# A top-64 attention kernel: VectorE writes the copy below the pivot and the final mask, GpSimd and the excess pass leave the group loop

## The reference, cut to what matters

```python
q = (x @ Wq)...; k, v = split(x @ Wkv)             # 16 heads of 64
k = concatenate([mem_k, k]); v = concatenate([mem_v, v])   # 16 memory columns ahead
dots = einsum('bhid,bhjd->bhij', q, k) * SCALE
dots = einsum('bhij,hk->bkij', dots, pre_proj)     # heads are mixed
dots = where(causal, NEG_INF, dots)
thresh = top_k(dots, 64)[0][..., -1:]              # the 64th largest of each row
dots = where(dots < thresh, NEG_INF, dots)
attn = softmax(dots, axis=-1)
out = einsum('bhij,bhjd->bhid', attn, v) ...
```

## Time and profile before

| | us |
|---|---|
| median of 3 runs (3874.14 to 3875.96) | 3874.56 |
| the profiled execution | 3873.98 |
| its span | 3872.1 |
| TensorE busy | 2315.0 |
| VectorE busy | 2245.1 |
| ScalarE busy | 1712.3 |
| GpSimd busy | 1674.8 |
| first pivots to the start of the last (63 periods) | 3137.5 |

### The profile page before, as it was taken

How to read it: one execution, slowest core, us unless ns; L and a number is a source line. 1 busy time by engine, 2 the same in 40 slices (tenths; PEclk the granted TensorE clock), 3 DMA queues, 4 the chain that set the end, 5 groups by cost and what they waited for, 6 DMA issues and landing times.

```text
span 3872.1 us, 34819 instructions
## 1 busy us (share of the span) xinstructions
PE 2315.0 (60%) x10182; PEld 1329.5 (34%) x10182; DVE 2245.1 (58%) x8918; ACT 1712.3 (44%) x2399; POOL 1674.8 (43%) x554
## 2 busy tenths in 40 slices
PE   5885445455556666336666675766660467673598
PEld 3553222233323333113333333333330234342365
DVE  3245776666665666775555555655579556451444
ACT  1212334444445555225555556555540555654221
POOL 0000233434455455235566557666640666757000
PEclk9896667777777878668787887888885788786799
DMA  1000000000000000000000000000000000000100
GB/s 46 1 1 1 1 1 1 1 1 1 1 1 1 1 1 1 0 1 1 1 1 1 1 1 1 1 1 1 1 1 0 1 1 1 1 1 1 38 1 11
DMA packets 15487, 12.02 MB, mean 3 GB/s; under 512 B 6892, under 2 KB 13686, under 8 KB 15222
## 3 DMA queue, kind: packets, MB, share of 16 engines
q1 hardware_dynamic: 11184, 6.82, 0.7%
q10 hardware_dynamic: 4038, 2.37, 0.2%
HBM read 8.14 MB, written 1.05 MB: 2 GB/s over the span
## 4 chain that ended last, share of the span: by engine, by line
DVE 35%; POOL 31%; PE 14%; issue 9%; ACT 8%; DVEq 3%; ACTq 0%; POOLq 0%
POOL F L425 26%; DVE W L1159 6%; POOL R L432 5%; DVE W L1160 4%; DVE r L1176 4%; DVE cand L1137 3%; PE bank L939 3%; DVE r L1208 3%; ACT R L566 3%; DVEq L1212 2%; ACT R L573 2%; DVE Pm L1221 2%; ACT R L558 2%; PE bank L947 2%; PE bank L857 1%
## 5 line engine op out<-in xcount | busy, mean ns | idle before, releaser
L425 POOL TENSOR_SCALAR F<-R,thr 128x144 bf16<-128x144 f32 (+15 forms) x256 | 1022.4, 3994 | 1246.8 <-DVEq L1171 1217.7
L841 PE MATMUL bank<-ident,R 128*128 128x128 f32 x2176 | 552.2, 327 | 1289.0 <-ACT R L573 1289.0
L432 POOL TENSOR_TENSOR R<-R 128x144 f32<-128x144 f32 (+15 forms) x256 | 647.2, 2528 | 655.3 <-ACT R L566 650.3
L841 PEld LDWEIGHTS bank<-ident,R 128*128 128x128 f32 x2176 | 356.5, 164 | 1540.7 <-issue 790.0
L857 PE MATMUL bank<-WP,Y 128*128 128x512 f32 x1088 | 667.6, 701 | 79.8 <-ACT WP L580 77.9
L573 ACT ACTIVATE R<-R,negm 128x144 f32<-128x144 f32 (+15 forms) x256 | 310.2, 1213 | 882.7 <-POOL F L425 882.0
L1137 DVE MAX8 cand<-R 128x8 f32<-128x12 f32 (+15 forms) x4096 | 558.7, 222 | 31.8 <-ACT R L543 13.0
L1176 DVE MAX8 r<-R 128x8 f32<-128x144 f32 (+15 forms) x256 | 334.0, 1306 | 404.6 <-POOL R L432 404.6
L825 PE MATMUL bank<-hT,qT 128*128 128x512 f32 (+3 forms) x1280 | 519.3, 540 | 28.9 <-ACT R L539 15.3
L842 PE MATMUL bank<-nidentb,F 128*128 128x128 bf16 x2176 | 484.3, 247 | 0.0
L543 ACT ACTIVATE R<-bank 128x1024 f32<-128x1024 f32 (+7 forms) x384 | 290.5, 774 | 379.2 <-PE bank L825 221.2
(11 more groups left out here) (219 smaller groups left out, 2287.4 us busy)
## 6 DMA issues: line engine op xcount, KB each, us to landing
R<-in_L_attn_Wkv ACTq DMA_DIRECT2D x2, 512.0 KB, 8.1
R<-in_L_ffn_gate_w SPq DMA_DIRECT2D x1, 1024.0 KB, 6.8
R<-in_L_ffn_up_w SPq DMA_DIRECT2D x1, 1024.0 KB, 9.4
out<-X SPq DMA_DIRECT2D x1, 1024.0 KB, 5.1
R<-in_L_attn_Wq ACTq DMA_DIRECT2D x1, 512.0 KB, 6.5
WP<-in_L_attn_Wo ACTq DMA_DIRECT2D x1, 512.0 KB, 10.9
R<-in_L_ffn_wi SPq DMA_DIRECT2D x1, 256.0 KB
R<-in_L_ffn_wo SPq DMA_DIRECT2D x1, 256.0 KB
```

The source lines that it names most:

```text
L425: pool.tensor_scalar(F[:, i, 0:n], S[:, k % NS, i, 0:n], thr[:, k % 2, i:i + 1], 4.0, ALU.is_lt, ALU.mult).then_inc(s_lose, 1)
L432: pool.tensor_tensor(A[:, u % 2, 0:n], S[:, p % NS, i, 0:n], A[:, u % 2, 0:n], ALU.subtract) .then_inc(s_below, 1)
L841: pe.transpose(to[:, P * i:P * i + P], S[:, k % NS, i, blk], ident[:, :])
```

## The change

GpSimd's loop and with it the semaphores `s_over`, `s_below` and `s_thr` are taken out; GpSimd keeps only the constants at the start. ScalarE's `excess` is taken out; its counts write their signs, which nobody reads, into row 0 of `A`. VectorE's `below` now writes the copy itself, in one instruction a tile: the score, less 1.0 where the score is above the cut. So that 1.0 is a huge number, all scores are scaled by `LOW` = 2^-30 through the constant `pre_b`, the causal mask is -1.0, `BIG_` goes to 2^90, and the exponential scales back. `r9` has the cut itself in front of the eight, so that a count of 64 has its threshold too; the tie term still looks at column 1, which now is the first of the eight. `threshold` ends with the four masks F, written by VectorE behind the branch. `memory_weights` moves ahead of the searches. On ScalarE all four exponentials come first, then three turns, then the four counts with a turn's drain behind each, then the other drains; the scores of group p+2 are drained at the end of iteration p (where those of p+1 were drained at its start).

The diff, without its changes of constants on GpSimd and of the branch's row of `A`:

```diff
@@ -19,16 +19,17 @@
 EPS = 1e-5
-FILL = -2.0 ** 30
+LOW = 2.0 ** -30
+FILL = -1.0
 NS = 3
 SC = 1024
-BIG_ = 2.0 ** 60
+BIG_ = 2.0 ** 90
 RANGE = 60000.0
...
 CUT = 56
-CONSTS = 3 + 2 * E0 + 9
+CONSTS = 4 + 2 * E0 + 9
 GU = 4
@@ -184,9 +185,9 @@
         W16 = sb("W16", [P, 2, 8 * CH * GU], F16)
-        r8 = sb("r8", [P, GU, 8])
-        hit = sb("hit", [P, GU, 8])
-        place = sb("place", [P, 8])
+        r9 = sb("r9", [P, GU, 9])
+        hit = sb("hit", [P, GU, 9])
+        place = sb("place", [P, 9])
         top = sb("top", [P, GU])
@@ -194,7 +195,7 @@
         idx = sb("idx", [P, GU])
-        thr = sb("thr", [P, 2, GU])
+        thr = sb("thr", [P, GU])
         tie = sb("tie", [P, GU])
@@ -310,10 +311,7 @@
         s_cnt = sem("s_cnt")
-        s_over = sem("s_over")
-        s_below = sem("s_below")
         s_eight = sem("s_eight")
-        s_thr = sem("s_thr")
         s_lose = sem("s_lose")
@@ -408,28 +407,6 @@
             pool.tensor_scalar(nidentb[:, :], ident[:, :], -1.0, None, ALU.mult).then_inc(s_const, 1)
-
-            for p in range(NG + 1):
-                if p >= 1:
-                    k = p - 1
-                    n = wide(k // 4)
-                    pool.wait_ge(s_thr, k + 1)
-                    if p < NG:
-
-                        pool.wait_ge(s_cut, p + 1)
-                    if k:
-
-                        pool.wait_ge(s_tfill, turned(k - 1))
-                        pool.wait_ge(s_pm, k)
-                    for i in range(GU):
-                        pool.tensor_scalar(F[:, i, 0:n], S[:, k % NS, i, 0:n], thr[:, k % 2, i:i + 1], 4.0, ALU.is_lt,
-                                           ALU.mult).then_inc(s_lose, 1)
-                if p < NG:
-                    n = wide(p // 4)
-                    for i in range(GU):
-                        u = GU * p + i
-                        pool.wait_ge(s_over, u + 1)
-                        pool.tensor_tensor(A[:, u % 2, 0:n], S[:, p % NS, i, 0:n], A[:, u % 2, 0:n], ALU.subtract)                            .then_inc(s_below, 1)
@@ -552,25 +529,17 @@
                 n = wide(k // 4)
-                if u >= 2:
-                    act.wait_ge(s_eight, u - 1)
+                if u:
+                    act.wait_ge(s_cnt, u)
                 act.wait_ge(s_cut, k + 1)
-                act.activation(A[:, u % 2, 0:n], S[:, k % NS, i, 0:n], ACT.Sign, bias=cutb[:, k % 2, i:i + 1], scale=BIG_,
+                act.activation(A[:, 0, 0:n], S[:, k % NS, i, 0:n], ACT.Sign, bias=cutb[:, k % 2, i:i + 1], scale=BIG_,
                                accum_out=cnt[:, k % 2, i:i + 1]).then_inc(s_cnt, 1)
-
-            def excess(k, i):
-
-                u = GU * k + i
-                n = wide(k // 4)
-                act.wait_ge(s_cnt, u + 1)
-                act.activation(A[:, u % 2, 0:n], S[:, k % NS, i, 0:n], ACT.Relu, bias=cutb[:, k % 2, i:i + 1], scale=BIG_)\
-                    .then_inc(s_over, 1)
...
                 row = S[:, k % NS, i, 0:n]
-                act.activation(row, row, ACT.Exp, bias=negm[:, k % 2, i:i + 1], scale=1.0).then_inc(s_prob, 1)
+                act.activation(row, row, ACT.Exp, bias=negm[:, k % 2, i:i + 1], scale=1.0 / LOW).then_inc(s_prob, 1)
@@ -590,29 +559,25 @@
             drain_scores(0)
+            drain_scores(1)
             for p in range(NG + 1):
-                if p + 1 < NG:
-                    drain_scores(p + 1)
+                turns = list(range((p - 1) // 4 + 1)) if p >= 1 else []
                 if p >= 1:
-                    exponent(p - 1, 0)
-                    exponent(p - 1, 1)
+                    for i in range(GU):
+                        exponent(p - 1, i)
+                    for j in turns[0:3]:
+                        drain_turn(p - 1, j)
                 if p < NG:
-                    count_above(p, 0)
-                    excess(p, 0)
+                    for i in range(GU):
+                        count_above(p, i)
+                        for j in turns[3 + i:4 + i]:
+                            drain_turn(p - 1, j)
                 if p >= 1:
-                    exponent(p - 1, 2)
-                    exponent(p - 1, 3)
-                turns = (p - 1) // 4 + 1 if p >= 1 else 0
-                ahead = [(f, i) for i in range(1, GU) for f in (count_above, excess)] if p < NG else []
-                for j in range(turns):
-                    while ahead and 10 * (7 - len(ahead)) <= 12 * j + 10:
-                        f, i = ahead.pop(0)
-                        f(p, i)
-                    drain_turn(p - 1, j)
-                for f, i in ahead:
-                    f(p, i)
-                if p >= 1:
+                    for j in turns[7 if p < NG else 3:]:
+                        drain_turn(p - 1, j)
                     drain_rest(p - 1)
+                if p + 2 < NG:
+                    drain_scores(p + 2)
@@ -1083,7 +1048,7 @@
                     dve.wait_ge(s_wa, 16 * 9)
-                    link(dve.tensor_scalar(pre_b, pre_b, DH ** -0.5, None, ALU.mult))
+                    link(dve.tensor_scalar(pre_b, pre_b, DH ** -0.5 * LOW, None, ALU.mult))
             dve.wait_ge(s_dve, done[0])
@@ -1141,8 +1106,8 @@
                 mark(dve.tensor_reduce(top[:, :], cand[:, 0].rearrange("p l u -> p u l"), AX.X, ALU.max))
-                link(dve.tensor_scalar(W16[:, 0, :], cand[:, :, :, :].rearrange("p r l u -> p (r l u)"), -RANGE, RANGE,
-                                       ALU.max, ALU.min))
+                link(dve.tensor_scalar(W16[:, 0, :], cand[:, :, :, :].rearrange("p r l u -> p (r l u)"), 1.0 / LOW, -RANGE,
+                                       ALU.mult, ALU.max))
                 flip, runs = 0, 8
@@ -1164,30 +1129,35 @@
                 link(dve.tensor_reduce(piv[:, :], dst.rearrange("p r u -> p u r"), AX.X, ALU.min))
-                mark(dve.tensor_scalar(negm[:, k % 2, :], top[:, :], -1.0, None, ALU.mult))
-                link(dve.tensor_scalar(cutt[:, :], piv[:, :], -BIG_ * (1 - NEAR), None, ALU.mult))
-                link(dve.scalar_tensor_tensor(out=cutb[:, k % 2, :], in0=piv[:, :], scalar=-BIG_ * (1 + NEAR),
+                mark(dve.tensor_scalar(negm[:, k % 2, :], top[:, :], -1.0 / LOW, None, ALU.mult))
+                link(dve.tensor_scalar(cutt[:, :], piv[:, :], -BIG_ * LOW * (1 - NEAR), None, ALU.mult))
+                link(dve.scalar_tensor_tensor(out=cutb[:, k % 2, :], in0=piv[:, :], scalar=-BIG_ * LOW * (1 + NEAR),
                                               in1=cutt[:, :], op0=ALU.mult, op1=ALU.max))
...
             def below(k, i):
-                u = GU * k + i
-                dve.wait_ge(s_below, u + 1)
-                dve.max(r8[:, i, :], A[:, u % 2, 0:wide(k // 4)]).then_inc(s_eight, 1)
+                u, n = GU * k + i, wide(k // 4)
+                row = S[:, k % NS, i, 0:n]
+                if i == 0:
+                    link(dve.tensor_scalar(r9[:, :, 0], cutb[:, k % 2, :], -1.0 / BIG_, None, ALU.mult))
+                link(dve.scalar_tensor_tensor(out=A[:, 1, 0:n], in0=row, scalar=r9[:, i, 0:1], in1=row, op0=ALU.is_gt,
+                                              op1=ALU.subtract, reverse1=True))
+                dve.max(r9[:, i, 1:9], A[:, 1, 0:n]).then_inc(s_eight, 1)
+                dve.wait_ge(s_eight, u + 1)
...
                 n = wide(t)
-                th = thr[:, k % 2, :]
+                th = thr[:, :]
                 dve.wait_ge(s_cnt, GU * k + GU)
...
                 link(dve.tensor_scalar(idx[:, :], cnt[:, k % 2, :], -0.5, TOPK - n / 2 + 0.25, ALU.mult, ALU.add))
-                mark(dve.scalar_tensor_tensor(out=tie[:, :], in0=r8[:, :, 1], scalar=-BIG_, in1=cutb[:, k % 2, :],
+                mark(dve.scalar_tensor_tensor(out=tie[:, :], in0=r9[:, :, 1], scalar=-BIG_, in1=cutb[:, k % 2, :],
                                               op0=ALU.mult, op1=ALU.is_le))
                 link(dve.tensor_scalar(idx[:, :], idx[:, :], HALF, -HALF, ALU.add, ALU.add))
-                link(dve.tensor_tensor(hit[:, :, :], place[:, :].unsqueeze(1).to_broadcast([P, GU, 8]), bc(idx[:, :], 8),
+                link(dve.tensor_tensor(hit[:, :, :], place[:, :].unsqueeze(1).to_broadcast([P, GU, 9]), bc(idx[:, :], 9),
                                        ALU.is_equal))
-                link(dve.tensor_tensor(hit[:, :, :], hit[:, :, :], r8[:, :, :], ALU.mult))
+                link(dve.tensor_tensor(hit[:, :, :], hit[:, :, :], r9[:, :, :], ALU.mult))
                 link(dve.tensor_reduce(th, hit[:, :, :], AX.X, ALU.add))
@@ -1203,16 +1173,21 @@
                     for i in range(GU):
-                        s_, a_, m_ = S[:, k % NS, i, 0:n], A[:, 0, 0:n], r8[:, i, :]
+                        s_, a_, m_ = S[:, k % NS, i, 0:n], A[:, 1, 0:n], r9[:, i, 1:9]
                         for r in range(8):
...
                                 dve.drain()
-                        dve.tensor_copy(thr[:, k % 2, i:i + 1], m_[:, 7:8])
+                        dve.tensor_copy(thr[:, i:i + 1], m_[:, 7:8])
```

(12 more changed lines are left out.)

5 lines of the change are left out of this document (3 added, 2 removed).

## The result

The changed kernel takes 3443.79 us (median of three runs, 3438.75 to 3448.46) against 3874.56 us: a ratio of 0.8887 with a 95% interval of 0.8867 to 0.8908, so 431 us less. The forecast was 3360 with a range of 3320 to 3500. The time lies 84 us above the forecast, on a rival with its price: one more exact search.

What follows compares the result with a forecast made beforehand. Hand-overs between engines, mainly VectorE and GpSimd, were taken to bound the kernel. VectorE's 2652 us, plus 30 for ScalarE and TensorE and 77 for the tail, gave a 2759 us loop against 3273.2, 514 less: 3360 us, range 3320 to 3500.

Steps and rivals of the forecast that it cites:

- the first rival: Exact-search branch: one score equal to the cut triggers it, some 45 to 145 us, 3455 and up; chance 0.32.
- What bounds it: Whole loop: hand-overs between engines, not a full engine (none busy over 60% of the span), bound the kernel before.
- VectorE's period: VectorE's steps for a group of four rows, n columns wide: 22.2 + 14/960 n us, 46.7 at 1680.
- The 34 us: VectorE between last search and next pivots: some 15 of 63 periods take 2.26 us more, 34 us in all.
- Pm at 0.21: L1221 on VectorE, moved ahead of the searches, takes 0.21 us; the other end is 1.46, 79 us more in all.
- The two old exact searches: Rare branch behind L1204, groups 34 and 55: both kernels take it there, 89.6 + 129.6 = 219 us.
- The case named likeliest: Whole kernel: the forecast of 3360 us, with exact searches in two groups only; chance 0.50.
- no single score equal to a cut: Flag's tie term: no row triggers another branch; 0.49 such rows expected in 32,768, chance 0.38 for one or more.
- The chain of ScalarE and TensorE: Exponentials, turns, counts, scores: 57.5 us at 2064 columns, 3.4 less a step, adding 30 us over the last four widths.
- The lower clock: TensorE at 0.50 through the counts: its chain binds from 1296 columns, about 95 us more, 3455; chance 0.07.
- The tail: From the last pivots to the end of the loop: 77 us, was 135.7.
- The sum: VectorE's 63 periods: 1399 + 1000 + 219 + 34 = 2652 us, plus 30 for ScalarE and TensorE.

Runs made afterwards that it cites:

- experiment 4b: Changed kernel with the masks F back on GpSimd and Pm behind the four copies and searches, ahead of the threshold: 3780.91 us, ratio 0.9758.
- experiment 5: Changed kernel with ScalarE's excess pass and GpSimd's subtraction making the copy again, F staying on VectorE and Pm early: 3731.22 us, ratio 0.963.
- experiment 1: Changed kernel with the tie term at column 2 of r9 again and no threshold ready for a count of 64: 3342.5 us, ratio 0.8624.
- experiment 3: Changed kernel without flag read and exact search, copy and top-8 search covering only the first half of each row: 2918.4 us, ratio 0.7534.
- experiments 4: Changed kernel with F on GpSimd again and Pm between the third and fourth search, the copy staying on VectorE: 3891.29 us, ratio 1.0045.
- experiment 2: Changed kernel with the flag neither read nor branched on, so without the exact search: 3031.04 us, ratio 0.7819.
- experiment 8: Changed kernel with the tie rule of before, plus the next group's fourth search moved between the flag and its reading: 3287.85 us, ratio 0.8486.

## Why the prediction was right, and where it was off

- **What bounds it.** Right. The stalls at the hand-overs went, not the sum of GpSimd's busy time. VectorE sets the period in 59 of 63, that is up to the third group at 1936 columns.
- **VectorE's period** (22.2 + 14n/960) held within 0.1 us in the plain groups of most widths: 26.1, 27.9, 29.8, 33.5, 37.3, 41.0, 44.7 and 46.6 us at 272, 400, 528, 784, 1040, 1296, 1552 and 1680 columns, against 26.2, 28.0, 29.9, 33.6, 37.4, 41.1, 44.8 and 46.7 by the sum. Copy and mask were priced from neighbours with another shape and pointer count, and both prices hold to 0.01 us. At 144 columns it didn't: 22.6 to 26.7 against 24.3. The 34 us for some 15 periods with 2.26 us more were about right: 13 of the 63 have 3.6 to 3.9 us from flag to mask where the others have 1.4, some 30 us.
- **Pm at 0.21** was right, with 0.226. The Trainium skill's rule on the shared port pair (SBUF — State Buffer, Who interferes with whom), which the forecast named beside this end, agrees: in the kernel before, the long Pm at 2590.32 ended at 2592.47 us, and the L432 that it met at 2592.38. Experiments 4b and 5 show other VectorE instructions that get longer beside GpSimd, in 4b by less than the rule has it.
- **The two old exact searches** stayed, in groups 34 and 55, as the count of scores above the pivots said. Their prices in the changed kernel are 91.3 and 131.0 us from flag to mask, beside the 91.06 and 131.09 to the pivots in the earlier trace rows.
- **The case named likeliest didn't happen.** The step that failed is "no single score equal to a cut", which had 0.50 against 0.32 for one or more. Group 40 has one, at 1424 columns, and pays 107.3 - 1.4 = 106 us. This was the first rival: its mechanism, with a price of 45 to 145 us by width, is what happened, and experiment 1 shows it by taking the term back. The range held because it took that rival in. Scores computed in double precision, as I had them, tell the counts above a cut but not whether the chip's own f32 scores come out equal to it.
- **The chain of ScalarE and TensorE** was mis-sized in what it adds. The forecast gave it 57.5 us at 2064 and 3.4 less a step, and added 30 us for the last four widths. Its own length was nearly right: experiment 3 shows means of 54.8, 53.0, 46.2 and 37.5 us at 2064, 1936, 1680 and 1296 columns, where the forecast's step gives 57.5, 54.1, 47.3 and 37.1. What it adds to the loop is some 14 us: one period of 54.1 at 1936, and 55.8, 55.4 and 57.8 at 2064 (the last with 2.3 of a slow flag read) against VectorE's 50.4 and 52.3. At 1808 it is 49.1 and not 50.7, so hardly longer than VectorE's 48.4. At 1936 it is 53.4 to 54.9 in the changed kernel too, but the exact search of group 55 had let ScalarE catch up, and the first three groups use that up. The forecast had no such term. The scores, taken as 18.3 us from the earlier trace rows, take 16.9 at 2064 (3039.47 to 3056.34). The stretch in the earlier trace rows has a drain of queries (L532, 0.60 us, and more wait for the next bank) among the scores; this one has none, and with one it is 18.2 at 1936 in both kernels. The whole is 55.5 where 57.5 was forecast.
- **The lower clock** was a rival if it lasted through the counts. It is 0.50 for some 10 us, from about 2 us after the start of the exponentials to just before the first count, and 1.00 from 3070 on, while the counts run. So only the first turns pay.
- **The tail** from the last pivots to the end of the loop was forecast at 77 us. The line that the earlier trace rows ends with is, in the changed kernel,

```profile
3186.98 3.19 DVE L941 BATCH_NORM_STATS2 st<-WP 128x6 f32<-128x128 f32 x16
```

  at 3186.98, 78.4 us after 3108.6.
- **The sum.** 63 periods: 2682 forecast, with the third search 2788, measured 2769.9; the 18 less are mostly the chain's 30, found as some 14. Outside the loop and in the tail the rest agrees within 2 us.
- **My expectations of experiments 4 and 5** failed by 190 and 250 us (and that of 4b by 80), far more than the forecast of the change itself. Both times I summed the engines' work and one wait, and didn't ask what was queued behind the waiting instruction: four copies behind Pm, and the turns' drains behind the counts.

So the gain doesn't split into a part for the mask and one for the copy. With the mask alone back on GpSimd the kernel takes 3781 to 3891 us, with the copy alone back 3731, with both in place but ScalarE's order taken back 3656. From 3875 to 3444 it takes all three; each half keeps one ring of hand-overs alive. These times all hold the third exact search, some 105 us that the kernel before hasn't. Less that, as an estimate, the change is worth 532 us (experiment 1), and with the mask back 87 to 198 of them are left, with the copy back 248, with ScalarE's order back 324.

## What to carry to other kernels

When an engine's work in a loop is cheap to redo on the engine that waits for it, price the move by the waits at the hand-over, not by busy times: here 537 us more work on VectorE (186.2 + 350.3) gave 431 us, and 532 without the third exact search. Ask for every wait that stays what stands behind it in its queue, on both engines. A fast path with a rare exact branch has to be costed with its trigger: a term that was loosened from two equal scores to one cost 101 us, almost a quarter of what the change gained. Such a search also stays in every comparison with the kernel before, until it is taken out of both sides.

## What the hardware showed that I had not expected

- Reading a flag into a register and branching costs VectorE 1.19 us of idle time in each group, and a little over 2 us more in 14 of the 64; both go when the branch goes (experiment 2). When another instruction of 2.8 us runs meanwhile, the 1.19 us go, but 1.1 to 2.6 us are left in 23 groups (experiment 8).
- A VectorE instruction of 128x4 elements took 1.18 us on average in experiment 5, up to 4.25 where it met GpSimd's two-input subtraction, and 0.16 without it. The Trainium skill (SBUF — State Buffer, Who interferes with whom) counts a TENSOR_SCALAR in a two-port mode among those that exclude GpSimd's, the one that starts first holding the ports for its whole length; the row agrees, since the instruction that began at 2693.08 ended 0.02 us after GpSimd's, though no run shows its mode. In 64 groups it is 65 us more.
- F as a TENSOR_SCALAR from f32 to bf16 with a pointer takes 1.09 us on VectorE and 5.93 on GpSimd for 1680 columns (the kernel before; 6.37 on average in experiment 4b, beside VectorE's copies).
